# Gated linear attention on Trainium2: decay groups arranged by block parity, with bounds kept as zeros in the decays

## What is computed

```python
def step(S, xs):
    q_t, k_t, v_t, g_t = xs
    S = jnp.exp(g_t)[:, :, None] * S + k_t[:, :, None] * v_t[:, None, :]
    o_t = jnp.einsum('bk,bkv->bv', q_t, S)
    return (S, o_t)
...
q = x @ Wq.T
k_sig = jax.nn.sigmoid(x @ Wk.T)
q = jax.nn.silu(q) * SCALE
gf = jax.nn.log_sigmoid(-k_sig)
o = _gla(q, k_sig, x, gf)
go = o @ Wog.T + x @ Wig.T
rms = o * jax.lax.rsqrt(jnp.mean(o * o, axis=-1, keepdims=True) + EPS) * g_weight
return rms * go * jax.nn.sigmoid(go)
```

## Time and profile before

| what | value |
|---|---|
| median of 3 runs | 983.83 us (983.77 to 985.61) |
| profiled execution, its own time | 985.32 us |
| span of its trace | 983.6 us |
| mean granted TensorE clock | 0.949 of full speed |
| busy in the span | PE 857.0, DVE 695.4, ACT 545.3, POOL 402.2 us |
| busy from 571 to 771 us (the GLA) | PE 152.9, DVE 169.1, ACT 118.5, POOL 158.0 us |

### The profile page before, as it was taken

How to read it: one execution, slowest core, us unless ns; L and a number is a source line. 1 busy time by engine, 2 the same in 40 slices (tenths; PEclk the granted TensorE clock), 3 DMA queues, 4 the chain that set the end, 5 groups by cost and what they waited for, 6 DMA issues and landing times.

```text
span 983.6 us, 21335 instructions
## 1 busy us (share of the span) xinstructions
PE 857.0 (87%) x7188; PEld 720.6 (73%) x7188; DVE 695.4 (71%) x1317; ACT 545.3 (55%) x1064; POOL 402.2 (41%) x464
## 2 busy tenths in 40 slices
PE   4599999999999997799999987777777569999997
PEld 3367667777667764688888977777776458888887
DVE  7566777777777774477676668988888636677765
ACT  3146454454545545566666666666666346666674
POOL 3822222222222234232322225889998642333320
PEclk9679999999999998899999998899999769999999
DMA  5755666566664532100000000000000000000001
GB/s 174 95 78 78 129 99 89 76 100 85 96 94 72 83 56 41 34 2 1 1 0 1 1 1 1 1 0 0 0 0 1 1 1 22 24 21 21 22 23 43
DMA packets 33751, 40.99 MB, mean 42 GB/s; under 512 B 4319, under 2 KB 25216, under 8 KB 33648
## 3 DMA queue, kind: packets, MB, share of 16 engines
q1 hardware_dynamic: 33690, 40.20, 24.3%
HBM read 9.25 MB, written 5.24 MB: 15 GB/s over the span
## 4 chain that ended last, share of the span: by engine, by line
PE 41%; DVE 25%; ACT 14%; issue 12%; DMA 2%; SPq 2%; POOL 2%; DVEq 1%; ACTq 1%; POOLq 0%
DVE inter L1765 5%; PE bank L406 5%; PE pair_a L834 5%; PE bank L407 4%; PE bank L408 4%; ACT stk L1383 4%; ACT gact L1388 4%; PE pair_b L815 3%; PE bank L848 3%; PE pair_b L807 3%; PE bank L1034 3%; DVE spline L1832 3%; DVE am_lo L1851 2%; PE bank L1044 2%; DVE in_lo L1770 2%
## 5 line engine op out<-in xcount | busy, mean ns | idle before, releaser
L581 POOL TENSOR_SCALAR_AFFINE_SELECT prob<-prob 128x512 f32<-128x512 f32 x128 | 82.2, 642 | 223.2 <-ACT prob L1259 223.2
L1259 ACT ACTIVATE prob<-pair_a 128x768 f32<-128x768 f32 x128 | 103.7, 810 | 98.3 <-PE pair_a L834 97.2
L406 PE MATMUL bank<-wd_hi,in_hi 128*128 128x256 f32 x512 | 147.7, 289 | 8.0 <-DVE X L1776 6.5
L1770 DVE TENSOR_TENSOR in_lo<-inter,in_hi 128x512 fp32r<-128x512 f32 x128 | 98.7, 771 | 78.8 <-ACT in_hi L1396 78.2
L408 PE MATMUL bank<-wd_hi,in_lo 128*128 128x256 f32 x512 | 142.9, 279 | 0.0
L407 PE MATMUL bank<-wd_lo,in_hi 128*128 128x256 f32 x512 | 142.8, 279 | 0.0
L1612 DVE TENSOR_REDUCE mx<-pair_b 128x6 f32<-128x768 f32 x124 | 118.0, 952 | 33.1 <-PE pair_b L815 32.5
L1396 ACT ACTIVATE in_hi<-inter 128x512 fp32r<-128x512 f32 x128 | 80.9, 632 | 94.6 <-DVE inter L1765 94.6
L1765 DVE TENSOR_TENSOR inter<-gact,pair_b 128x512 f32<-128x512 f32 x128 | 87.6, 684 | 48.8 <-ACT gact L1388 48.7
L406 PEld LDWEIGHTS bank<-wd_hi,in_hi 128*128 128x128 f32 x512 | 97.1, 190 | 16.2 <-issue 5.7
L407 PEld LDWEIGHTS bank<-wd_lo,in_hi 128*128 128x128 f32 x512 | 97.5, 191 | 3.6
(11 more groups left out here) (242 smaller groups left out, 2360.6 us busy)
## 6 DMA issues: line engine op xcount, KB each, us to landing
stack<-stage SPq DMA_DIRECT2D x192, 128.0 KB, 4.7
result<-X SPq DMA_DIRECT2D x8, 512.0 KB, 2.9
X<-in_attn_a_x SPq DMA_DIRECT2D x14, 256.0 KB, 5.0
stack<-mrow SPq DMA_DIRECT2D x128, 4.0 KB
wdx<-spline SPq DMA_DIRECT2D x1, 1024.0 KB
wd_lo<-wdx SPq DMA_DIRECT2D x16, 64.0 KB
spline<-factor_basis SPq DMA_DIRECT2D x1, 1008.0 KB, 7.1
win<-decay_windows SPq DMA_DIRECT2D x1, 672.0 KB, 7.3
```

The costliest lines, as they stand in the source:

```text
L406: pe.matmul(dst, l_hi, r_hi, start=first, stop=False)
L1259: act.activation(prob[:, p % 4], pair_a[:, :, P:4 * P], ACT.Exp, scale=DK ** -0.5).then_inc(a_e, 1)
L1770: dve.tensor_tensor(in_lo[:, m % LAG, :], inter[:, m % 2, :], in_hi[:, m % LAG, :].bitcast(F32), ALU.subtract).then_inc(f_.il, 1)
```

## The change

The seven groups become five, in partitions 0, 16, 32 (decays towards tokens 64, 192 and 128) and 64, 96 (even and odd blocks of 64). The 112 rows stay, two gaps of 16 are zero. Where a running product has to end, `dec` holds a zero that is set once and never overwritten, so the windows on POOL go, and with them the tiles `qwn`, `kwn`, `dq`, `dk`. ACT writes `dec` in three pieces around those zeros; DVE reads `qs`, `ks` and `dec` directly; `g_activate(n)` now waits for `g_.kd` of sample n-1. The backward scan adds before it multiplies. The reciprocal is taken in two pieces of 16 partitions. The products are three of 128x128 (9 matmuls in place of 6), the empty fourth (later keys, earlier queries) is not made, and mask, `am`, `am_hi`, `am_lo` have 384 columns in place of 512. No engine's order of calls within a period changes, except that POOL's `g_windows` is gone. The hunks not shown here resize tiles, drop `f.w` and POOL's calls of `g_windows`, copy the projection weights into five groups on ACT as on DVE, index `am_hi` and `am_lo` by their three parts in `g_output`, and rename the table.

```diff
@@ -49,8 +49,11 @@
-NG = 7
-GR = NG * KG
+GROUPS = (0, 16, 32, 64, 96)
+CROSS = 48
+NEAR = (64, 96)
+GR = 112
+AM = 3 * P
@@ -124,35 +127,25 @@
-def decay_windows():
-    w = np.zeros((GR, 6, S), np.float32)
-    run, start, krun, kstart, qwin, kwin = (w[:, n] for n in range(6))
-    for g in range(4):
+def decay_starts():
+    w = np.zeros((GR, 2, S), np.float32)
+    for g, ref in ((0, 64), (1, 192), (2, 128)):
...
-        run[r] = 1.0
-        run[r, ::64] = 0.0
-        start[r, ::64] = GROW
-        qwin[r, 64 * g:64 * g + 64] = 1.0
-        kwin[r, 64 * g:64 * g + 64] = KG ** -0.5
-    for g, ref, length in ((4, 64, 64), (5, 192, 64), (6, 128, 128)):
-        r = slice(KG * g, KG * g + KG)
-        run[r, ref + 1:ref + length] = 1.0
-        start[r, ref] = 1.0
-        krun[r, ref - length:ref] = 1.0
-        kstart[r, ref] = 1.0
-        qwin[r, ref:ref + length] = 1.0
-        kwin[r, ref - length:ref] = KG ** -0.5
+        w[r, 0, ref] = 1.0
+        w[r, 1, ref - 1] = 1.0
+    for h in range(2):
+        w[NEAR[h]:NEAR[h] + KG, 0, 64 * h::P] = GROW
@@ -676,20 +670,6 @@
-            def g_windows(n):
-                pool.wait_ge(g_.qs, upto(g_.qs, n, 1))
-                pool.wait_ge(g_.qd, upto(g_.qd, n - 1, 1))
-                pool.tensor_tensor(qwn, qs, win[:, 4], ALU.mult).then_inc(g_.w, 1)
-                pool.wait_ge(g_.ks, upto(g_.ks, n, 1))
-                pool.wait_ge(g_.kd, upto(g_.kd, n - 1, 1))
-                pool.tensor_tensor(kwn, ks, win[:, 5], ALU.mult).then_inc(g_.w, 1)
-                pool.wait_ge(g_.de, upto(g_.de, n, 1))
-                pool.wait_ge(g_.sf, upto(g_.sf, n - 1, 1))
-                pool.tensor_tensor(dq, dec, win[:, 0], ALU.mult).then_inc(g_.w, 1)
-                pool.wait_ge(g_.sb, upto(g_.sb, n - 1, 1))
-                pool.tensor_tensor(dk[:, 0:S - 1], dec[:, 1:S], win[:, 2, 0:S - 1], ALU.mult).then_inc(g_.w, 1)
@@ -740,13 +717,13 @@
-            pool.memset(causal01[:, :, :], 1.0).then_inc(s_gc, 1)
+            pool.memset(causal01[:, :], 1.0).then_inc(s_gc, 1)
...
-            pool.affine_select(out=causal01[:, 0, 0:P], in_=causal01[:, 0, 0:P], compare_op=ALU.is_ge, fill=0.0,
-                               base=0, pattern=[[1, P]], channel_multiplier=-1).then_inc(s_gc, 1)
-            pool.affine_select(out=causal01[:, 1, :], in_=causal01[:, 1, :], compare_op=ALU.is_ge, fill=0.0,
-                               base=-P, pattern=[[1, S]], channel_multiplier=-1).then_inc(s_gc, 1)
-            pool.memset(dk[:, S - 1:S], 0.0).then_inc(s_gc, 1)
+            for at in (0, 2 * P):
+                pool.affine_select(out=causal01[:, at:at + P], in_=causal01[:, at:at + P], compare_op=ALU.is_ge,
+                                   fill=0.0, base=0, pattern=[[1, P]], channel_multiplier=-1).then_inc(s_gc, 1)
+            pool.memset(dec, 0.0).then_inc(s_gc, 1)
+            pool.memset(fk, 0.0).then_inc(s_gc, 1)
@@ -1117,10 +1094,10 @@
-                for t in range(TB):
-                    keys = slice(P * t, P * t + P)
-                    i = mm3(pe, pair_a[:, 0, S * t:S * t + S], qk_hi[:, 1, keys], qk_lo[:, 1, keys],
-                            qk_hi[:, 0, :], qk_lo[:, 0, :], True, True)
+                for at, rows, k, q in ((0, GR, 0, 0), (P, CROSS, 0, 1), (2 * P, GR, 1, 1)):
+                    k, q = slice(P * k, P * k + P), slice(P * q, P * q + P)
+                    i = mm3(pe, pair_a[:, 0, at:at + P], qk_hi[0:rows, 1, k], qk_lo[0:rows, 1, k],
+                            qk_hi[0:rows, 0, q], qk_lo[0:rows, 0, q], True, True)
@@ -1443,14 +1420,19 @@
             def g_activate(n):
...
-                act.wait_ge(g_.w, upto(g_.w, n - 1, 4))
+                act.wait_ge(g_.kd, upto(g_.kd, n - 1, 1))
                 act.activation(kt, bank_p[0:GR, S:2 * S], ACT.Tanh, scale=0.5).then_inc(g_.kt, 1)
                 act.activation(qs, bank_p[0:GR, 0:S], ACT.Silu).then_inc(g_.qs, 1)
...
                 act.activation(dt, kt, ACT.Tanh, bias=quarter[0:GR, :], scale=0.25).then_inc(g_.dt, 1)
-                act.activation(ks, kt, ACT.Copy, bias=0.5, scale=0.5).then_inc(g_.ks, 1)
+                act.activation(ks, kt, ACT.Copy, bias=0.5 * KG ** -0.5, scale=0.5 * KG ** -0.5).then_inc(g_.ks, 1)
...
-                act.activation(dec, dt, ACT.Copy, bias=0.5, scale=-0.5).then_inc(g_.de, 1)
+                for rows, cut in (((0, 32), P), ((32, CROSS), 0), ((NEAR[0], GR), 64)):
+                    to, of = dec[rows[0]:rows[1]], dt[rows[0]:rows[1]]
+                    if cut:
+                        to, of = (v.rearrange("p (w s) -> p w s", s=cut)[:, :, 1:] for v in (to, of))
+                    i = act.activation(to, of, ACT.Copy, bias=0.5, scale=-0.5)
+                i.then_inc(g_.de, 1)
@@ -1534,6 +1516,7 @@
                 if m == 5:
+                    act.wait_ge(s_gc, 6)
@@ -1582,10 +1565,13 @@
             def low_gla_weights():
-                dve.wait_ge(s_prep_hi, 6 + NG)
+                dve.wait_ge(s_prep_hi, 6 + len(GROUPS))
...
-                for g in range(NG):
-                    cols = slice(KG * g, KG * g + KG)
+                for part in (wqk_hi, wqk_lo):
+                    for gap in (CROSS, NEAR[0] + KG):
+                        dve.memset(part[:, :, :, gap:gap + KG].bitcast(F32), 0.0)
+                for g in GROUPS:
+                    cols = slice(g, g + KG)
@@ -1821,19 +1807,26 @@
             def g_scans(n):
-                dve.wait_ge(g_.w, upto(g_.w, n, 4))
-                dve.wait_ge(g_.qd, upto(g_.qd, n - 1, 1))
-                dve.tensor_tensor_scan(fq, dq, win[:, 1], 0.0, ALU.mult, ALU.add).then_inc(g_.sf, 1)
-                dve.tensor_tensor_scan(fk[64:GR, ::-1], dk[64:GR, ::-1], win[64:GR, 3, ::-1], 0.0, ALU.mult,
-                                       ALU.add).then_inc(g_.sb, 1)
+                dve.wait_ge(g_.de, upto(g_.de, n, 1))
+                dve.wait_ge(g_.kd, upto(g_.kd, n - 1, 1))
+                dve.tensor_tensor_scan(fq, dec, win[:, 0], 0.0, ALU.mult, ALU.add).then_inc(g_.sf, 1)
+                dve.tensor_tensor_scan(fk[0:CROSS, S - 2::-1], win[0:CROSS, 1, S - 2::-1], dec[0:CROSS, S - 1:0:-1],
+                                       0.0, ALU.add, ALU.mult).then_inc(g_.sb, 1)
             def g_decayed(n):
                 dve.wait_ge(g_.sf, upto(g_.sf, n, 1))
-                dve.reciprocal(fk[0:64], fq[0:64]).then_inc(g_.rc, 1)
+                for h in range(2):
+                    near = slice(NEAR[h], NEAR[h] + KG)
+                    f, t = (v[near].rearrange("p (t h s) -> p h t s", h=2, s=64)[:, h] for v in (fk, fq))
+                    i = dve.reciprocal(f, t)
+                i.then_inc(g_.rc, 1)
+                dve.wait_ge(g_.qs, upto(g_.qs, n, 1))
                 dve.wait_ge(g_.qkh, upto(g_.qkh, n - 1, 1))
-                dve.tensor_tensor(qk[:, 0], qwn, fq, ALU.mult).then_inc(g_.qd, 1)
+                dve.tensor_tensor(qk[:, 0], qs, fq, ALU.mult).then_inc(g_.qd, 1)
+                dve.wait_ge(g_.sb, upto(g_.sb, n, 1))
+                dve.wait_ge(g_.ks, upto(g_.ks, n, 1))
                 dve.wait_ge(g_.rc, upto(g_.rc, n, 1))
-                dve.tensor_tensor(qk[:, 1], kwn, fk, ALU.mult).then_inc(g_.kd, 1)
+                dve.tensor_tensor(qk[:, 1], ks, fk, ALU.mult).then_inc(g_.kd, 1)
...
                 dve.wait_ge(g_.qkh, upto(g_.qkh, n, 1))
@@ -1843,12 +1836,12 @@
-                dve.scalar_tensor_tensor(out=am, in0=pair_a[:, 0, :].rearrange("p (k t) -> p k t", k=TB), scalar=BIG,
-                                         in1=causal01[:, :, :], op0=ALU.min, op1=ALU.mult).then_inc(g_.am, 1)
+                dve.scalar_tensor_tensor(out=am, in0=pair_a[:, 0, 0:AM], scalar=BIG, in1=causal01[:, :], op0=ALU.min,
+                                         op1=ALU.mult).then_inc(g_.am, 1)
             def g_low_am(n):
...
-                dve.tensor_tensor(am_lo[:, :, :], am, am_hi[:, :, :].bitcast(F32), ALU.subtract).then_inc(g_.aml, 1)
+                dve.tensor_tensor(am_lo[:, :], am, am_hi[:, :].bitcast(F32), ALU.subtract).then_inc(g_.aml, 1)
```

More of the change, by code:

```diff
@@ L124, in spline_features @@
             np.ascontiguousarray(moments.astype(np.float32)))
-def decay_windows():
-    w = np.zeros((GR, 6, S), np.float32)
-    run, start, krun, kstart, qwin, kwin = (w[:, n] for n in range(6))
-    for g in range(4):
+def decay_starts():
+    w = np.zeros((GR, 2, S), np.float32)
+    for g, ref in ((0, 64), (1, 192), (2, 128)):
         r = slice(KG * g, KG * g + KG)
-        run[r] = 1.0
-        run[r, ::64] = 0.0
-        start[r, ::64] = GROW
-        qwin[r, 64 * g:64 * g + 64] = 1.0
-        kwin[r, 64 * g:64 * g + 64] = KG ** -0.5
-    for g, ref, length in ((4, 64, 64), (5, 192, 64), (6, 128, 128)):
-        r = slice(KG * g, KG * g + KG)
-        run[r, ref + 1:ref + length] = 1.0
-        start[r, ref] = 1.0
-        krun[r, ref - length:ref] = 1.0
-        kstart[r, ref] = 1.0
-        qwin[r, ref:ref + length] = 1.0
-        kwin[r, ref - length:ref] = KG ** -0.5
+        w[r, 0, ref] = 1.0
```

(23 more changed lines are left out.)

14 lines of the change are left out of this document (5 added, 9 removed).

## The result

The changed kernel takes 1009.48 us (median of 4 runs, 1006.78 to 1012.78) against 984.72 for the kernel before (4 runs, 983.77 to 985.68): a ratio of 1.0253, 95% interval 1.0217 to 1.0289, so +24.8 us. The forecast was 1006.5 with a range of 994 to 1021.

A forecast was written before the change was run, and what follows sets the result against it. DVE was taken to set the pace: cycle 4.43 + 1.98 + 6.9 = 13.31 us, 1.60 more, times 15 is 24.0, less 1.3 gives +22.7. That made 1008.0 profiled, 1.5 lower as median: 1006.5 us, range 994 to 1021.

The forecast's parts named there:

- the first part of the cycle: From T, the end of the key multiplication, to the first scan: forecast 6.41 us, 1.98 later than before.
- The new wait: Between key multiplication and L1840: ACT's activations move from slack into the path, 2.13 us before `qk_hi` starts.
- the step of a piece of `dec`: In ACT's activations: a copy follows a copy after 0.30 us; upper bound 0.41 for each extra piece.
- rival B: PE becomes the bound at a lower granted clock, deciding above 0.186 us per matmul: +15, 1021.5 us; chance 0.13.
- From the scan to the key multiplication: From first scan to end of L1836: DVE alone 5.6 us, with POOL's residual 6.9, in place of 7.28.
- DVE's order: Behind the scan: L1851 is ready at 1.43 us; where it is first, POOL ends L708 at 6.2 to 6.3.
- The reciprocal in two pieces: On DVE between scan and L1836: two halves take 1.70 us, one piece 1.67.
- The lock: Two-input DVE instructions and POOL's SBUF reads exclude each other: L1834 stands for POOL, 1.31 us in place of 0.35.
- rival C: DVE and POOL only slow each other: part behind the scan 6.3 us, cycle 12.7, total 998 us; chance 0.22.
- hidden both ways: Before L1846: the nine product matmuls take 1.1 or 1.7 us, by clock, within 2.4 us available.
- The small terms: First cycle 1.3 us less, without POOL's residual; POOL's windows, its memsets and pieces before the attention cost nothing.
- nobody waits for them: POOL's four windows: removing them counted as nothing extra, their effect on DVE being counted in the other terms.

## Why the prediction was right, and where its steps were off

Sign, mechanism and range held, and the time was 3.0 us too low. In the profiled execution the fifteen cycles took 201.2 us where 198.4 were forecast, and the 1.98 ahead of them are not in the sum. Part of the nearness is luck: the first part of the cycle came out 10.4 us above its forecast in all, and the second 7.5 below. Term by term:

- **The new wait.** Right in its place: L1424 starts 0.09 after T and L1833 waits 3.28, forecast 2.8. The mis-sized term is the step of a piece of `dec`, taken as 0.30 from the earlier trace rows and measured at 0.42; the upper bound of 0.41 was nearly exact. The block lasts 2.52 instead of 2.13. With the 0.09 it puts the scan at T + 6.88 at least, where 6.41 was forecast, 7.2 us in fifteen cycles. Of the other 3.2 us, 1.5 are the last cycle's, which the sum left out by taking 4.43 for every cycle. In eight cycles some 1.7 to 1.8 more are added: 0.6 where DVE waits for ACT's squares for up to 0.5 in place of 0.24, and the rest by PE, as told under rival B.
- **From the scan to the key multiplication.** Forecast 6.9, measured 6.42 to 6.51 in full cycles. L680 starts 1.53 after the scan (forecast 1.51). The step that failed is DVE's order: with scans of 0.60 and 0.58 from start to start instead of 0.71 and 0.72, L1844 is ready at 1.18 rather than 1.43 and through before POOL is held up, so POOL ends at 5.89, not at 6.2. The reciprocal in two pieces went the other way: 1.94 from its start to the next, not 1.70. Where L1825 stands for POOL in any case, that costs nothing.
- **The lock.** L1825 stands until POOL's L688 is done, with a median of 1.08 us where about 1.3 was forecast, and takes 0.42 without the residual. In eleven cycles it starts 0.42 to 0.64 after L688 and ends 0.28 after it each time; in the last three L1829, starting 0.02 to 0.03 after L688, takes 1.53 to 1.55 and ends 0.28 after it too. A mere slowing, as in rival C, would not tie the end to POOL's. The Trainium skill, page "SBUF — State Buffer", section "Who interferes with whom", says that issue order decides who blocks; the two kinds of cycle in the run with the products alone agree (0.69 against 1.63 for the same scan). The run with the windows put back does not wholly: there L671 goes ahead of a scan that started before it and already stood.
- **Rival B.** Its premise came true: over the fifteen cycles the granted clock was 0.78, against 0.89 before, and in the first 0.61. The matmuls took 0.165 us each on average (158.28 by 962), below the 0.186 from which B was to decide, and it did not decide. But the forecast's "hidden both ways" for the nine products failed. In five cycles, from 691 to 759 us, they ran at a granted clock of 0.50, the lower of its two levels, and took 2.53 to 2.56 us, not 1.1 to 1.7, in the 2.4 that they were given. Two stretches from the first to the last product, with the columns of the earlier trace rows, and L1839 in the cycle of the second:

```profile
682.43:683.94 1.51, 1.51 (x9) 1.22 (x9) 0.49 (x2) 1.51 (x5) 1.08 (x2) 1.00 0.00 0
709.41:711.97 2.56, 2.56 (x10) 2.17 (x10) 1.46 (x3) 2.19 (x7) 1.95 (x2) 0.50 0.00 0
```

```profile
712.00 0.56 DVE L1839 SCALAR_TENSOR_TENSOR spline<-pair_a,causal 128x384 f32<-128x384 f32 x1
```

In these five cycles L1839 starts 0.04 to 0.13 us behind the end of the products, and 0.70 to 0.82 behind the start of the instruction before it, instead of 0.60: 0.9 us in all. The first cycle loses 0.2 on balance, though L1839 waits 1.06 for PE there, because DVE has fewer instructions ahead of it. That is 1.1 us of the 15 that B was priced at. In the two-buffer kernel the products take 1.49 to 1.51 us in every cycle but the first.
- **The small terms.** The first cycle was to be 1.3 shorter than the others and is 0.4 shorter. Behind its scan it takes 5.90, 0.3 more than forecast and only 0.6 less than a full cycle, since the full ones came out shorter; ahead of it PE's wait adds 0.2. The forecast's "nobody waits for them" of POOL's windows was true to the word, and yet putting them back cost 17.7 us, in the part behind the scan (7.52 instead of 6.33 on average).

The first scan is 0.68 in all 16 cycles, as forecast. Medians of one line each, in ns min/median/max:

```profile
L1825 DVE TENSOR_TENSOR spline<-spline x16: 426/1079/1155, 597.5 to 797.2; 112x256 f32<-112x256 f32 x16
```

```profile
L1434 ACT ACTIVATE spline<-spline x48: 397/409/418, 581.4 to 787.3; 32x254 f32<-32x254 f32 x16, 16x256 f32<-16x256 f32 x16, 48x252 f32<-48x252 f32 x16
```

## What to carry to other kernels

Where a stage is dropped from between two engines, look at what the tile's new last reader is: the writer inherits its wait, and everything in the writer's program behind that wait moves with it; a second buffer here turned +24.8 us into -13.2. Price removed work on an engine that makes another stand by what it held up and not by who waited for it, and once the cycle is short, move work that depends on nothing near into the gap that is left.

## What was not expected of the hardware

Three copies on ACT of 32, 16 and 48 partitions took 0.41 us each, as one of 112 partitions does, and followed each other after 0.42, while a copy followed another activation of 112 partitions after 0.30 and `qk_hi` followed the undivided `dec` after 0.31. Why successive pieces don't overlap as the whole ones do was not tried.

Matmuls of 128 columns are hardly cheaper than those of 256. PE's products in one cycle after, and then in one before, the granted clock being 1.00 in both stretches:

```profile
641.97 0.33 PE L400 MATMUL pair_a<-qk_hi 112*128 112x128 f32 x1 [2.36 <-DVE qk_lo L1833]
642.14 0.28 PE L401 MATMUL pair_a<-qk_lo,qk_hi 112*128 112x128 f32 x1
...
642.45 0.32 PE L400 MATMUL pair_a<-qk_hi 48*128 48x128 f32 x1
...
643.21 0.27 PE L402 MATMUL pair_a<-qk_hi,qk_lo 112*128 112x128 f32 x1
```

```profile
655.66 0.39 PE L406 MATMUL pair_a<-qk_hi 112*128 112x256 f32 x1 [0.68 <-DVE qk_lo L1840]
...
656.36 0.28 PE L408 MATMUL pair_a<-qk_hi,qk_lo 112*128 112x256 f32 x1
```

Nine take 1.51 us from first start to last end, six of twice the width 0.98: a quarter fewer columns cost half as much time again. At a granted clock of 1.00 this lay beside other work; at 0.50 it did not, as told above. Why the clock is at the lower level during the products from the eighth to the twelfth cycle, and not from the second to the seventh, with the same work in each, is open.

The two scans follow each other after 0.60 us in the changed kernel and after 0.71 in the kernel before, where POOL is not beside them, at the same 0.68 for the first. The second differs in its partitions, its length and the order of its operations; which of these counts stays open.
